# The scan's input of the first chunk kept in PSUM, and the preparation of later chunks moved behind each scan

## What is computed

```
xp    = x @ W_xproj.T                     # 64 ranks, 16 columns of B, 16 of C
delta = softplus(xp[:, :64] @ W_dt.T + b_dt)
A     = -exp(A_log)
h     = h * exp(delta * A) + x * delta * B      # step by step in time
y     = sum over n of h * C
x     = x + y + x * D
```

## Time and profile before

| | |
|---|---|
| median of 3 runs | 331.68 us (331.42 to 332.87) |
| the profiled execution's own time | 332.46 us |
| its span | 330.6 us |
| VectorE busy | 263.3 us, 80% of the span |
| TensorE busy | 264.2 us, 80% |
| GpSimd busy | 192.4 us, 58% |
| ScalarE busy | 131.3 us, 40% |
| mean granted TensorE clock | 0.917 of full |

### The profile page before, as it was taken

How to read it: one execution, slowest core, us unless ns; L and a number is a source line. 1 busy time by engine, 2 the same in 40 slices (tenths; PEclk the granted TensorE clock), 3 DMA queues, 4 the chain that set the end, 5 groups by cost and what they waited for, 6 DMA issues and landing times.

```text
span 330.6 us, 4799 instructions
## 1 busy us (share of the span) xinstructions
PE 264.2 (80%) x1432; PEld 188.6 (57%) x1432; DVE 263.3 (80%) x618; ACT 131.3 (40%) x270; POOL 192.4 (58%) x152
## 2 busy tenths in 40 slices
PE   5789999649749977976697258689999999999820
PEld 3335444225326433543446136579999999999810
DVE  1699599999999999999999889684887887555333
ACT  3175796305433443343311300143553554654410
POOL 1454926599747664656572502777567777772640
PEclk9996799759998997999899659999999999999985
DMA  8005002526940001000100200224243343320168
GB/s 233 8 1 127 0 2 66 125 45 153 284 167 21 0 0 31 0 0 0 32 0 0 86 12 8 51 48 122 73 127 101 100 145 93 108 80 26 45 187 230
DMA packets 23958, 24.28 MB, mean 73 GB/s; under 512 B 2752, under 2 KB 17408, under 8 KB 23936
## 3 DMA queue, kind: packets, MB, share of 16 engines
q1 hardware_dynamic: 18752, 17.53, 18.9%
q0 software_dynamic: 2560, 5.25, 6.1%
q10 hardware_dynamic: 2624, 1.24, 1.4%
HBM read 13.00 MB, written 6.82 MB: 60 GB/s over the span
## 4 chain that ended last, share of the span: by engine, by line
PE 44%; DVE 24%; issue 11%; POOL 8%; ACT 5%; DMA 5%; DVEq 1%; ACTq 1%; POOLq 0%; SPq 0%
PE psum L1544 11%; DVE ring L550 6%; PE psum L1523 5%; PE psum L1525 5%; PE psum L1524 5%; POOL ring L1177 5%; DVE psum L540 4%; PE psum L1370 3%; PE psum L1332 3%; PE psum L1286 2%; DMA small<-in_small 1%; PE psum L1276 1%; POOL parts L1162 1%; PE psum L1497 1%; DMA ring<-pairs 1%
## 5 line engine op out<-in xcount | busy, mean ns | idle before, releaser
L1177 POOL TENSOR_TENSOR ring<-ring,cbc 128x1024 f32<-128x1024 f32 x31 | 73.1, 2361 | 43.7 <-DVE ring L550 42.4
L1332 PE MATMUL psum<-stack,sel_r 128*128 (+1 forms) x120 | 50.8, 522 | 25.1 <-DVE ring L550 23.1
L1370 PE MATMUL psum<-ring,cst 128*128 128x512 f32 x128 | 66.4, 647 | 0.9 <-POOL ring L1177 0.9
L550 DVE TENSOR_TENSOR_SCAN ring<-ring,psum 128x1024 f32<-128x1024 f32 x25 | 57.1, 2285 | 1.6
L1231 POOL DMA_INDIRECT ring<-rows,gid x40 | 38.8, 971 | 31.3 <-issue 24.8
L982 ACT ACTIVATE ring<-psum,nega 128x510 f32<-128x510 f32 x64 | 40.4, 680 | 36.7 <-PE psum L1332 34.8
L1332 PEld LDWEIGHTS psum<-stack,sel_r 128*128 128x128 f32 x120 | 22.1, 201 | 51.2 <-DVE ring L550 23.5
L1241 POOL DMA_INDIRECT pairs<-ring,sid x40 | 40.1, 1004 | 18.8 <-issue 15.4
L859 DVE TENSOR_TENSOR ring<-psum,ring 128x320 f32<-128x320 f32 x64 | 31.3, 491 | 21.9 <-ACT ring L1088 17.0
L1088 ACT ACTIVATE ring<-psum 128x320 f32<-128x320 f32 x64 | 27.9, 437 | 38.0 <-PE psum L1525 38.0
L1523 PE MATMUL psum<-stack 128*128 128x320 f32 x128 | 40.9, 319 | 0.5 <-ACT ring L1088 0.5
(11 more groups left out here) (187 smaller groups left out, 357.1 us busy)
## 6 DMA issues: line engine op xcount, KB each, us to landing
stack<-parts SPq DMA_DIRECT2D x16, 256.0 KB, 3.8
pairs<-zero SPq DMA_DIRECT2D x1, 2048.0 KB, 12.3
win_s<-in_wg SPq DMA_DIRECT2D x8, 256.0 KB, 3.2
win_s<-in_w SPq DMA_DIRECT2D x8, 256.0 KB, 3.9
w_s<-in_w SPq DMA_DIRECT2D x8, 256.0 KB, 2.8
ring<-pairs SPq DMA_DIRECT2D x6, 256.0 KB, 4.1
xt<-in_x SPq DMA_DIRECT2D x4, 256.0 KB, 4.4
rows<-xn SPq DMA_DIRECT2D x4, 256.0 KB, 2.3
```

What stands on the lines that cost most here:

```text
L550: v.tensor_tensor_scan(hh[:, s].rearrange("p a b -> p (a b)"), da[:, s].rearrange("p a b -> p (a b)"), inputs.rearrange("p a b -> p (a b)" ...
L1177: g.tensor_tensor(hc[:, s], hh[:, s], cb, ALU.mult).then_inc(s_product, 1)
L1332: ins = mm(bank(to), sel, stack[:, half, kind, bass.ts(c, CH)], start=True, stop=True)
L1370: ins = mm(bank(YB), wred[:, o:o + D], hc[:, s, k, :], start=(grp == 0), stop=(grp == NG - 1))
```

## The change

In the first chunk `u_step` now writes where it reads, in PSUM, always on banks 2 and 3, and the scan reads its input there. Those banks come free only when the scan is over, so TensorE waits for `s_state` before X(v+1). The scan follows its own `u_step` at once, and `positive` and `delta` stand behind the scan. TensorE spreads D(v+1) at the head of step v and X(v+1) at its end. B's rows of the three later chunks are copied by ScalarE instead of VectorE.

```diff
-        def input_bank(vv):
-
-            return SPREAD_X + UG * ((vv + 1) % 2)
+        def input_bank(c, vv):
+
+            return SPREAD_X if isinstance(c, int) and c == 0 else SPREAD_X + UG * ((vv + 1) % 2)
...
-            def u_step(c, vv, to_ring=False):
+            def u_step(c, vv):
                 for k in range(UG):
-                    n, m = c * UPC + vv, c * NG + (UG * vv + k)
+                    m = c * NG + (UG * vv + k)
                     dve.wait_ge(s_dx_spread, m + 1)
-                    if to_ring and k == 0 and above_zero(n - (RING - 1)):
-                        dve.wait_ge(s_state, n - (RING - 1))
-                    b = input_bank(vv) + k
-                    dst, src = (uu[:, vv % RING, k, :], bank(SPREAD_X + k)) if to_ring else (bank(b), bank(b))
-                    v.tensor_tensor(dst, src, bbc[:, bass.ts(c, CH)], ALU.mult).then_inc(s_input, 1)
+                    b = input_bank(c, vv) + k
+                    v.tensor_tensor(bank(b), bank(b), bbc[:, bass.ts(c, CH)], ALU.mult).then_inc(s_input, 1)
...
-                inputs = uu[:, s] if from_ring else psum[:, b:b + UG, :]
+                inputs = psum[:, b:b + UG, :]
...
             def first_chunk():
                 dve.wait_ge(s_delta, 1)
+
                 for vv in range(UPC):
-                    u_step(0, vv, vv < UPC - 1)
-                    if vv < 2:
-                        scan_step(0, vv, True)
+                    u_step(0, vv)
+                    scan_step(0, vv)
                     if vv == 0:
                         for j in range(3 * TPC, NT):
                             normalise(j)
                     if 2 <= vv < NC + 1:
                         positive(vv - 1)
                     if NC <= vv < 2 * NC - 1:
-                        b_rows(vv - NC + 1)
                         delta(vv - NC + 1)
-                        dve.wait_ge(s_b, vv - NC + 2)
-                    if vv > 2:
-                        scan_step(0, vv - 1, True)
-                scan_step(0, UPC - 1)
+                dve.wait_ge(s_b, NC)
...
+            def b_rows(c):
+
+                act.wait_ge(s_bc_product, 2 * c + 1)
+                a.activation(bbc[:, c * CH:(c + 1) * CH], bank(BB[c]), ACT.Copy).then_inc(s_b, 1)
+
...
                         if NC <= vv < 2 * NC - 1:
+                            b_rows(vv - NC + 1)
                             c_rows(vv - NC + 1)
                             high(vv - NC + 1)
...
-            def spread(vv):
+            def first_spread(vv, kinds=(0, 1)):
 
                 for k in range(UG):
                     m = UG * vv + k
-                    for kind, (to, used) in enumerate(((SPREAD_D, s_decay), (SPREAD_X, s_input))):
-                        if above_zero(m - 1):
-                            pe.wait_ge(used, m - 1)
-                        spread_group(0, m, kind, to + k, vv < DIRECT)
+                    for kind in kinds:
+                        if kind == 0 and m > 1:
+                            pe.wait_ge(s_decay, m - 1)
+                        if kind == 1 and vv:
+                            pe.wait_ge(s_state, vv)
+                        spread_group(0, m, kind, (SPREAD_D, SPREAD_X)[kind] + k, vv < DIRECT)
...
             def first_chunk():
+                first_spread(0)
                 for vv in range(UPC):
-                    if vv == DIRECT:
+                    if vv + 1 == DIRECT:
                         pe.wait_ge(s_stack, STACKED)
-                    spread(vv)
+                    if vv + 1 < UPC:
+                        first_spread(vv + 1, (0,))
...
                     if vv >= LAG:
                         reduce(0, vv - LAG)
+                    if vv + 1 < UPC:
+                        first_spread(vv + 1, (1,))
```

More of the change, by code:

```diff
@@ L530, in _, with scan_step @@
             dve.wait_ge(s_b, 1)
-            def u_step(c, vv, to_ring=False):
+            def u_step(c, vv):
                 for k in range(UG):
-                    n, m = c * UPC + vv, c * NG + (UG * vv + k)
+                    m = c * NG + (UG * vv + k)
                     dve.wait_ge(s_dx_spread, m + 1)
-                    if to_ring and k == 0 and above_zero(n - (RING - 1)):
-                        dve.wait_ge(s_state, n - (RING - 1))
-                    b = input_bank(vv) + k
-                    dst, src = (uu[:, vv % RING, k, :], bank(SPREAD_X + k)) if to_ring else (bank(b), bank(b))
-                    v.tensor_tensor(dst, src, bbc[:, bass.ts(c, CH)], ALU.mult).then_inc(s_input, 1)
-            def scan_step(c, vv, from_ring=False):
+                    b = input_bank(c, vv) + k
+                    v.tensor_tensor(bank(b), bank(b), bbc[:, bass.ts(c, CH)], ALU.mult).then_inc(s_input, 1)
+            def scan_step(c, vv):
                 n, s = c * UPC + vv, vv % RING
-                b = input_bank(vv)
-                inputs = uu[:, s] if from_ring else psum[:, b:b + UG, :]
+                b = input_bank(c, vv)
+                inputs = psum[:, b:b + UG, :]
                 dve.wait_ge(s_input, n * UG + UG)
@@ L1347, in spread_input @@
                 for k in range(UG):
-                    spread_group(c, UG * vv + k, 1, input_bank(vv) + k)
+                    spread_group(c, UG * vv + k, 1, input_bank(c, vv) + k)
             def spread_decay(c, vv):
```

## The result

| | before | changed |
|---|---|---|
| median | 332.2 us (331.42 to 332.87, 4 runs) | 337.62 us (336.07 to 341.17, 4 runs) |
| ratio | | 1.0148, 95% interval 1.0101 to 1.0196 |
| span of the profiled execution | 330.6 us | 335.7 us |
| second chunk's first `u_step` | 72.44 us | 77.56 us |
| start of the last scan | 167.82 us | 172.77 us |

The changed kernel is slower, by about 5 us (1.5% of 332). One of its four executions, the one of 341.17 us, was in a slower state (a mean granted clock of 0.889, the others 0.914 to 0.918), and the ratio leaves it out. The first chunk ends 5.1 us later, the last scan starts 4.95 us later and the span is 5.1 us longer: all of it is lost in the first chunk, and next to nothing changes behind it.

The account below looks back on a forecast made before the run. TensorE was taken to bound the first chunk up to u(3), VectorE from there. Followed in time, the second chunk starts at 76.1 against 72.44, 3.7 us more: 331.7 + 3.7 = 335.4 us, range 331.0 to 338.0.

Parts of the forecast that it names:

- scans at 2.3 us throughout: First chunk, VectorE: scans reading PSUM are no longer held up beside GpSimd; 3.0 us saved.
- B's copies off VectorE: First chunk: three copies leave VectorE, each moving the next instruction by 0.60 us; 1.8 us saved, free on ScalarE.
- idle ahead of scan(4): First chunk: VectorE waits for decay(4), behind ScalarE's late absolute value, tables and logarithms; 3.7 us.
- `delta` behind scan(6): Late first chunk: L494 waits 0.7 us for a low part, GpSimd's next product holds L497 for 2.2; 4.3 us.
- my full value: Late first chunk: `delta`'s last block is held for as long as GpSimd's product, 2.36 us less the signal, 2.2.
- the smaller limit of 1.31 us: Alternative for that hold: the longest block of a VectorE row before; sum 0.9 us smaller, 334.5.
- the second rival: First chunk: new TensorE idle gaps lengthen its half-clock stretch; 337.3 us, at most 338.5; 14%.
- the gain of 4.8 us: First chunk, VectorE: saving from unheld scans (3.0 us) and B's copies moved away (1.8 us).
- the ledger: Check of the first chunk's sum: 12.2 us added minus 8.1 saved, 4.1, against the 3.7 taken.
- the third rival: First chunk: VectorE stays the bound, 4.8 us saved, absolute value before about 42.3; 327.9 us, 10%.
- The early clock: First chunk, step 1: TensorE's full clock returns near 31 us, 3.0 us less; 332.4 us, 12%.
- VectorE as the bound, the faster case: The same as the third rival: decay(4) done at 49.2 when u(4) ends; 3.8 us faster, 10%.

Follow-up runs that it names:

- e12: The changed kernel unedited, measured again in the session of e9 to e11; 339.61 us, ratio 1.0214.
- e1: The kernel before, with only the copies of B's rows moved from VectorE to ScalarE; 332.79 us, ratio 0.9994.
- e2_d_late: The changed kernel with D(v+1) put behind its step's transposes, `outer`, `inner` and B's and C's rows; 334.03 us, ratio 1.0007.
- e4_both: The changed kernel with D(v+1) late and decay(4) ahead of ScalarE's tables and logarithms; 331.9 us, ratio 0.9959.
- e8_all: e7_decays_ahead with u(0) alone written to SBUF, X(1) waiting for it instead of scan(0); 329.92 us, ratio 0.9921.
- e7_decays_ahead: e4_both with decay(5) to decay(7) ahead of the high parts on ScalarE; 330.57 us, ratio 0.9966.
- e5_busy_in_wait: The changed kernel with 34 matmuls that nobody reads filling TensorE's wait ahead of D(5); 336.15 us, ratio 1.0105.
- e6: e4_both with `delta` between `u_step` and scan again; 330.94 us, ratio 0.9941.
- e9: e8_all with `delta` between `u_step` and scan; 330.41 us, ratio 0.9944.
- e3: The changed kernel with decay(4) moved ahead of the table loads and logarithms on ScalarE; 339.94 us, ratio 1.0124.
- e11: The changed kernel with u(0) alone written to SBUF, X(1) not waiting for scan(0); 339.35 us, ratio 1.0175.
- e10: e3 with u(0) alone written to SBUF, X(1) not waiting for scan(0); 335.58 us, ratio 1.0126.

## Why the prediction was right

Forecast 335.4 us, slower; measured 337.62, or about 5 us more than before where I had 3.7. The second session's 339.61 (e12) lies above the range, so that the time fell into it was in part luck. The steps, one by one:

| step | forecast | measured |
|---|---|---|
| scans at 2.3 us throughout | 3.0 us saved | all 32 at 2.29 |
| B's copies off VectorE | 1.8 us saved | 0 by itself (e1) |
| u(2) | 37.9 | 38.61 |
| u(3) | 42.7 | 43.14 |
| absolute value, last chunk | 46.0 | 46.45 |
| idle ahead of scan(4) | 3.7 | 3.61 |
| scan(4) | 52.9 | 53.44 |
| end of scan(5) | 61.3 | 63.99 |
| waits ahead of scan(6), scan(7) | 0.8 each | 0.69, 0.70 |
| `delta` behind scan(6) | 4.3 | 3.9 (69.47 to 73.38) |
| second chunk's start | 76.1 | 77.56 |

**What held.** The chain was read rightly from the order and the durations. D's place is the largest part (e2_d_late: 3.8 us from u(2) on, 1.5 of them behind scan(4), where the clock was kept), decay(4)'s place the second (1.9 us in e4_both), X(1)'s wait for scan(0) the third (1.3 us of the start in e8_all, nearly half of it the clock's), the order of decays 5 to 7 the fourth (0.8 us in e7_decays_ahead). Some 0.5 us more came from executions that were ahead or behind at u(2) for no reason of an edit; together this is the way from 77.56 to 69.28. It is more than the loss of 5.1 us, which is why the repaired version (e8_all) comes out below the old kernel. The rule cited from the Trainium skill ("SBUF — State Buffer", section "Who interferes with whom"), by which a hold lasts as long as GpSimd's instruction, agrees with this trace: L497 at 70.78 took 2.67 us, 2.0 over its usual 0.69, so my full value was better than the smaller limit of 1.31 us.

**What was mis-sized.** The term is the stretch behind scan(4), in which I let X(5) be ready when `delta` was over and put a wait of 0.8 us ahead of scan(5). TensorE had stood idle 4.09 us, the clock fell at 52.2 within that time, u(5) waited 2.60 us, and scan(5) then waited for nothing. I had put this cold stretch only into the second rival, which was thus half true. From next start to next start, the 1.46 us between 76.1 and 77.56 add up like this:

| stretch | forecast | measured | difference |
|---|---|---|---|
| to the end of scan(4) | 55.1 | 55.64 | +0.54 |
| scan(4) to scan(5) | 6.2 | 8.26 | +2.06 |
| scan(5) to scan(6) | 6.3 | 5.57 | -0.73 |
| scan(6) to the second chunk | 8.5 | 8.09 | -0.41 |

The first is what is left of the later rise of the clock (38.5 instead of 37) and of rounding. The last two are `delta`: the one behind scan(5), for which I had counted a hold by GpSimd, was not held (0.67 and 0.69 us), and the one behind scan(6) took 3.9 us instead of 4.3. They went the other way; without them the start would have been 2.6 us later than forecast. Filling the idle time gave 1.5 us back in e5_busy_in_wait.

**A saving that was none.** I counted B's copies as 1.8 us saved, since each moved the next start by 0.60 us. In the kernel before they bought nothing: e1_b_rows_only shows L494 longer by just that. The 76.1 us do not rest on this term, for they were followed in time with the copies absent; the gain of 4.8 us, the ledger and the 327.9 of the third rival do. Without it the ledger's saving is 3.0 us for the scans, and no run prices these alone either. In the changed kernel, where `delta` stands behind other work, no run put the copies back, so what they are worth there stays open.

**The rivals.** The early clock did not happen in any run. VectorE as the bound, the faster case, needed the absolute value before 42.3 us; it came at 46.45. The nearest thing to it is e8_all, where it came at 42.40, decay(4) was early by its own place, and 3.2 us of the start were gained, 2.3 us of the median.

What stays open is how often an execution gets its clock back late. The kernels that keep D late had it back between 37 and 40 us in each of their profiles (e2, e4, e6 to e9), though three of them lost it again behind 59 us (e4, e8, e9); of those that have D first, two had it back at 53 to 54 (e3, e11), one at 41 (e12), and three at 38.5 to 39.6 (the changed kernel, e5, e10), two of which lost it again between 45 and 50 (e5, e10). One profile each is no frequency.

## What to carry to other kernels

Moving a producer's work ahead of other work is only early if what it waits for is early too: D(v+1) at the head of the step waited for decays that ScalarE had not reached yet, behind the copy of the last `inner` and once behind the tables and logarithms, and the work that it was moved past waited with it. A one-step lag between a product and its scan can be slack (argued here, not tested by itself); before taking it away, look for the longest block on the engine that feeds the scan, here two table loads and three logarithms. And before a freed instruction is counted as a saving, look at what the next one on that engine does when it starts earlier: in e1 a held instruction just grew by the same amount. Last, before two profiles are subtracted, compare them at a point that the edit cannot have reached; here that took over a third off the price of decay(4)'s place.

## What the runs showed of the hardware

- TensorE stayed at half clock through nearly unbroken work: from 40 to 52 us it was busy for 11.90 of 12.00 us at 0.50 in e3_decay4_early, the same in e11_u0_ring. With the spreads behind the transposes and projections (e2_d_late) it was back near 39.7 us. The Trainium skill ("TensorE: Matmul & The Clock Gate", section "Part 1: The HAM clock gate") says that activity releases the throttle; busy time as the profile gives it did not do so here.
- In e5_busy_in_wait the clock fell at 46.5 us, in work, 2.2 us behind the end of a wait of only 0.89 us.
- Holding goes both ways and alternates: L494 holds a product for 0.45 us (2.81 instead of 2.36), and the product holds L497 for 2.0 us.
- A VectorE instruction held by GpSimd counts as busy, so the 9.90 of 10.00 us of the kernel before (50 to 60 us) were no measure of VectorE's own work: L494 took up to 2.02 us in e1_b_rows_only where a free one takes 0.67.
